# Four-layer graph network on one core: both edge counts inside the first sort, layer 0's gathers in three parts, its softmax by chunks

## The reference

```python
h = x @ W_lin + b_lin                         # 6250 x 128, 4 heads of 32
alpha = leaky_relu(h[src]·att_i + h[dst]·att_j + b_att, 0.2)   # 100000 x 4
amax = segment_max(alpha, src)
ex = exp(alpha - amax[src])
attn = ex / (segment_sum(ex, src) + 1e-16)    # softmax over the edges of one source
out = segment_sum(h[src] * attn, dst)
```

## Time and profile before

| | us |
|---|---|
| median of 3 runs | 8602.71 (8601.63 to 8605.87) |
| the profiled execution | 8623.17 |
| its span, first to last instruction | 8621.3 |

### The profile page before, as it was taken

One profiled execution on the slowest core, in us unless ns is written; L12 is line 12 of the kernel. 1 busy time (PEld: TensorE's weight loads), 2 busy tenths in 40 slices (PEclk: granted clock), 3 DMA queues, 4 the chain that ended last, 5 costly groups with the idle time before them and its releaser, 6 DMA issues. The chain is left out here.

```text
span 8621.3 us, 28596 instructions
## 1 busy us (share of the span) xinstructions
PE 941.1 (11%) x3526; PEld 575.1 (7%) x3526; DVE 4022.7 (47%) x9756; ACT 694.6 (8%) x1670; POOL 5185.7 (60%) x5176
## 2 busy tenths in 40 slices
PE   5301001310000000000004555100000001000000
PEld 4300000210000000000002222000000001000000
DVE  6881111954253443333333666667433335435445
ACT  0020000210000001000002333000000003000002
POOL 0077776023677675767664666663667775767673
PEclk9999999655555555555556877555555555555555
DMA  1070000000233333323232676431223331333332
GB/s 44 35 279 2 2 2 1 0 17 23 82 105 96 100 101 94 98 86 100 86 95 83 239 245 243 146 102 50 87 86 94 92 97 60 88 85 102 88 95 58
DMA packets 283027, 772.97 MB, mean 90 GB/s; under 512 B 112213, under 2 KB 116235, under 8 KB 269395
## 3 DMA queue, kind: packets, MB, share of 16 engines
q0 software_dynamic: 166160, 284.56, 14.7%
q1 hardware_dynamic: 98632, 378.76, 11.5%
q10 hardware_dynamic: 18040, 107.82, 3.2%
HBM read 359.19 MB, written 411.57 MB: 89 GB/s over the span
## 5 line engine op out<-in xcount | busy, mean ns | idle before, releaser
L569 POOL DMA_INDIRECT first_sj<-scores,prep_atdst x784 | 816.4, 1041 | 657.0 <-POOLq L59 401.1
L947 POOL DMA_INDIRECT l2z_rows<-proj,l2z_idx x784 | 786.9, 1004 | 425.6 <-issue 240.3
L1978 POOL DMA_INDIRECT l2s_krow<-table_k,l2s_idx x784 | 774.5, 988 | 417.1 <-issue 257.1
L947 POOL DMA_INDIRECT l3z_rows<-table,l3z_idx x784 | 791.2, 1009 | 339.1 <-issue 236.8
L947 POOL DMA_INDIRECT l1z_rows<-table,l1z_idx x784 | 786.5, 1003 | 327.1 <-issue 238.7
L947 POOL DMA_INDIRECT l0z_rows<-table,l0z_idx x784 | 776.3, 990 | 337.7 <-issue 232.3
L923 DVE SCALAR_TENSOR_TENSOR l2z_acc<-l2z_acc,g_dokeep,l2z_msg 128x128 f32<-128x128 f32 x784 | 278.4, 355 | 657.5 <-DVE l2z_acc L923 303.9
L923 DVE SCALAR_TENSOR_TENSOR l1z_acc<-l1z_acc,g_dokeep,l1z_msg 128x128 f32<-128x128 f32 x784 | 277.8, 354 | 591.6 <-DVE l1z_acc L923 291.6
L1933 PE MATMUL l2s_bank<-l2o_wr,l2s_fed 128*128 128x512 f32 x800 | 423.3, 690 | 300.8 <-ACT l2s_fed L1957 217.3
L1915 DVE SCALAR_TENSOR_TENSOR l2s_qrow<-l2s_qrow,g_dokeep,l2s_zrow 128x82 f32<-128x82 f32 x1568 | 368.0, 301 | 185.7 <-DVE l2s_qrow L1915 118.8
L923 DVE SCALAR_TENSOR_TENSOR l0z_acc<-l0z_acc,g_dokeep,l0z_msg 128x128 f32<-128x128 f32 x784 | 277.3, 354 | 274.5 <-DVE l0z_acc L923 148.6
(11 more groups left out here) (595 smaller groups left out, 3748.6 us busy)
## 6 DMA issues: line engine op xcount, KB each, us to landing
proj<-l2s_proj ACTq DMA_DIRECT2D x100, 1024.0 KB
spread_q<-prep_zero SPq DMA_DIRECT2D x98, 656.0 KB
l2s_zrow<-spread_q SPq DMA_DIRECT2D x98, 656.0 KB
prefix<-l3z_acc SPq DMA_DIRECT2D x98, 520.0 KB
prefix<-l0z_acc SPq DMA_DIRECT2D x98, 512.0 KB
prefix<-l1z_acc SPq DMA_DIRECT2D x98, 512.0 KB
prefix<-l2z_acc SPq DMA_DIRECT2D x98, 512.0 KB
first_sj<-scores,prep_atdst POOLq DMA_INDIRECT x784
```

The costliest lines, as they stand in the source:

```text
L569: nc.gpsimd.indirect_dma_start(out=sj[:, j, :], out_offset=None, in_=g.scores0, in_offset=bass.IndirectOffsetOnAxis(ap=at_dst[:, j:j + 1], ...
L947: nc.gpsimd.indirect_dma_start(out=rows[:, r, u, :], out_offset=None, in_=table, in_offset=bass.IndirectOffsetOnAxis(ap=idx[:, k * U + u:k ...
L1978: nc.gpsimd.indirect_dma_start(out=krow[:, h, u, :], out_offset=None, in_=g.table_k, in_offset=bass.IndirectOffsetOnAxis(ap=idx[:, h, u:u ...
```

## The change

1. **Counts.** Both tallies (`src` and `dst`) run in the first sort's turns, with rings of 2 (`RING2`) in place of 4. The digits, the zero memsets and the step table move from ahead of the network into its first turn (`later(0)`). Both raw arrays are loaded there. The second sort has no tally, no raw load and no digits.
2. **Loads in parts.** The 97 or 127 row loads are cut into 96 + 1 or 112 + 15 rows. The 96-row parts of `src` and `dst` don't wait for a memset. x goes by ACT's queue in parts of 96, 16 and 13 rows, the last two behind a memset that is now POOL's.
3. **Gathers of sj in three parts.** 560 columns (`BESIDE`) beside the second sort, 124 more (up to `SPREAD` = 684) at the start of a new block, then both spreads (100 scatters and 2 gathers), then the last 100.
4. **One block `source_softmax`** replaces the ten or so blocks between the second sort and the sum: positions, marks (forwards only), node ends, spreads, and a softmax with a running maximum and total by five chunks of columns (`FETCHED`), each when its gathers have landed. A scan within each partition gives running maxima; exp of the differences rescales the running total. `CarryStats` joins the partitions at the end: one row per partition is gathered from `stats`, corrected and scattered back. Then 50 node gathers in groups of 4. `table0` goes out in two parts, the first (h and si) at the block's start.
5. `ROW0` is 140 instead of 144; the scores si are stored too (`scores_i`); `stats` has 129 rows more; SP fills two more small tables (`rowed`).

The diff, cut to its core:

```diff
-ROW0 = 144
+ROW0 = D + 3 * HEADS
...
+RING2 = 2
...
+    def digits(self, eng, chain, key, hi, lo):
+        v = self.nc.vector
+        eng.wait_ge(*self.loaded)
+        chain(v.tensor_copy(key, self.raw))
+        rounded(v, chain, hi, key, 1.0 / NB, -(NB - 1) / 2.0 / NB)
+        chain(v.scalar_tensor_tensor(lo, hi, -float(NB), key, ALU.mult, ALU.add))
+        v.tensor_copy(self.hi[:], hi)
+        chain(v.tensor_copy(self.lo[:], lo))
...
-            if c >= 4:
-                eng.wait_ge(self.tallied, c - 3)
+            if c >= RING2:
+                eng.wait_ge(self.tallied, c - RING2 + 1)
...
+                nc.gpsimd.memset(g.x[96:P], 0.0).then_inc(cleared, 1)
+                pool.wait_ge(cleared, 1)
...
-                v.memset(g.zero[:], 0.0)
-                v.memset(g.x[96:P], 0.0).then_inc(ready, 1)
...
+                def later(t):
+                    if t == 0:
+                        v.memset(g.zero[:], 0.0).then_inc(ready, 1)
+                        v.memset(g.zmat[:], 0.0).then_inc(zeroed, 1)
+                        v.memset(g.eps[:], 1e-5)
+                        eng.wait_ge(io, 3)
+                        chain(v.tensor_copy(g.steps[:], isteps[:]))
+                        for tally in tallies:
+                            tally.digits(eng, chain, fkey[:], hi[:], lo[:])
+                    for tally in tallies:
+                        tally.offer(eng, t)
+
+                net.on_vector(eng, later)
...
+                flat = a["x"].rearrange("(p b) f -> p b f", b=NB)
+                act.dma_start(g.x[0:96], flat[0:96]).then_inc(nodes, 16)
+                act.wait_ge(cleared, 1)
+                act.dma_start(g.x[96:112], flat[96:112]).then_inc(nodes, 16)
+                act.dma_start(g.x[112:NREAL], flat[112:NREAL]).then_inc(nodes, 16)
...
+                for k in range(2):
+                    sp.dma_start(wide[0:96, k, :], load[k][0:96]).then_inc(edges, 16)
...
+                for k in range(2):
+                    by_row = arrays[k][0:EFULL * NC].rearrange("(p j) -> p j", j=NC)
+                    for lo, hi in ((0, 112), (112, EFULL)):
+                        sp.dma_start(raw[lo:hi, k, :], by_row[lo:hi]).then_inc(plain, 16)
...
+                sp.dma_start(by_nodes(g.scores_i), rows[:, :, D:D + HEADS]).then_inc(sis, 16)
...
-                for j in range(NC):
-                    nc.gpsimd.indirect_dma_start(out=sj[:, j, :], out_offset=None, in_=g.scores0,
-                                                 in_offset=bass.IndirectOffsetOnAxis(ap=at_dst[:, j:j + 1], axis=0)).then_inc(got[j % 2], 16)
-                for h in range(2):
-                    pool.wait_ge(got[h], 16 * NC // 2)
+                fetch_columns(nc, g, at_dst, sj, got, 0, BESIDE)
...
-                net.on_vector(eng, lambda t: tally.offer(eng, t))
-                tally.take(eng, count)
+                net.on_vector(eng, lambda t: None)
...
+FETCHED = [0, 392, 560, 684, 756, NC]
+BESIDE, SPREAD = 560, 684
+
+
+def fetch_columns(nc, g, at_dst, sj, got, lo, hi):
+    for c, (a, b) in enumerate(zip(FETCHED, FETCHED[1:])):
+        for j in range(max(a, lo), min(b, hi)):
+            nc.gpsimd.indirect_dma_start(out=sj[:, j, :], out_offset=None, in_=g.scores0,
+                                         in_offset=bass.IndirectOffsetOnAxis(ap=at_dst[:, j:j + 1], axis=0)).then_inc(got[c], 16)
...
+    def on_pool(self, pool):
+        where = self.order.lead_i
+        self.nc.gpsimd.indirect_dma_start(out=self.row[:], out_offset=None, in_=self.g.stats,
+                                          in_offset=bass.IndirectOffsetOnAxis(ap=where[:, 0:1], axis=0)).then_inc(self.lead, 16)
+        pool.wait_ge(self.fixed, 1)
+        self.nc.gpsimd.indirect_dma_start(out=self.g.stats, out_offset=bass.IndirectOffsetOnAxis(ap=where[:, 0:1], axis=0),
+                                          in_=self.row[:], in_offset=None).then_inc(self.sent, 16)
+        pool.wait_ge(self.sent, 16)
...
+            @block.gpsimd
+            def _(pool):
+                nc.gpsimd.iota(nid_i[:], pattern=[[1, NB]], base=EP, channel_multiplier=NB).then_inc(io, 1)
+                fetch_columns(nc, g, at_dst, sj, got, BESIDE, SPREAD)
+                for k, (order, table, node) in enumerate(((so, g.spread_s, lambda b: rows[:, b, D:D + HEADS]),
+                                                          (O.dst, g.spread_0, lambda b: rows[:, b, D + HEADS:D + 2 * HEADS]))):
+                    pool.wait_ge(named, k + 1)
+                    for b in range(NB):
+                        nc.gpsimd.indirect_dma_start(out=table, out_offset=bass.IndirectOffsetOnAxis(ap=order.start_i[:, b:b + 1], axis=0),
+                                                     in_=node(b), in_offset=None).then_inc(sent[k], 16)
+                for k, table in enumerate((g.scores_i, g.scores0)):
+                    nc.gpsimd.indirect_dma_start(out=init[:, k], out_offset=None, in_=table,
+                                                 in_offset=bass.IndirectOffsetOnAxis(ap=firsts[:, k:k + 1], axis=0)).then_inc(started[k], 16)
+                fetch_columns(nc, g, at_dst, sj, got, SPREAD, NC)
+                pool.wait_ge(stored, 16 * len(chunks))
+                carry.on_pool(pool)
+                for k, group in enumerate(GROUPS):
+                    for b in group:
+                        nc.gpsimd.indirect_dma_start(out=nodes[:, b, :], out_offset=None, in_=g.stats,
+                                                     in_offset=bass.IndirectOffsetOnAxis(ap=so.end_i[:, b:b + 1], axis=0)).then_inc(taken[k], 16)
...
+                for c, (lo, hi) in enumerate(chunks):
+                    m = hi - lo
+                    e, x0, x1 = sj[:, lo:hi, :], x[:, 0, 0:m], x[:, 1, 0:m]
+                    most, total = both[:, 1 + lo:1 + hi, HEADS:8], both[:, 1 + lo:1 + hi, 0:HEADS]
+                    if c == 2:
+                        eng.wait_ge(loaded[1], 16)
+                        eng.wait_ge(started[1], 16)
+                        for w in range(HEADS):
+                            chain.add(v.tensor_tensor_scan(sj_d[:, w, :], O.dst.keep[:], wide0[:, :, w], init[:, 1, w:w + 1], ALU.mult, ALU.add))
+                    eng.wait_ge(got[c], 16 * m)
+                    chain(v.tensor_tensor(e, e, si[:, lo:hi], ALU.add))
+                    chain(v.scalar_tensor_tensor(e, e, 0.2, e, ALU.mult, ALU.max))
+                    for w in range(HEADS):
+                        chain.add(v.tensor_tensor_scan(most[:, :, w], gap[:, lo:hi], e[:, :, w], both[:, lo, HEADS + w:HEADS + w + 1], ALU.add, ALU.max))
+                    chain.until()
+                    chain.add(v.tensor_tensor(x1, e, most, ALU.subtract))
+                    chain(v.tensor_tensor(x0, both[:, lo:hi, HEADS:8], bc_last(gap[:, lo:hi], HEADS), ALU.add))
+                    v.tensor_tensor(x0, x0, most, ALU.subtract).then_inc(asked, 1)
+                    eng.wait_ge(made, c + 1)
+                    for w in range(HEADS):
+                        v.tensor_tensor_scan(total[:, :, w], x0[:, :, w], x1[:, :, w], both[:, lo, w:w + 1], ALU.mult, ALU.add).then_inc(scanned, 1)
+                    eng.wait_ge(scanned, HEADS * (c + 1))
+                v.tensor_copy(ends[:], both[:, NC]).then_inc(known, 1)
+                carry.on_vector(eng, chain)
...
+                sp.dma_start(by_nodes(g.table0)[:, :, 0:D + HEADS], rows[:, :, 0:D + HEADS]).then_inc(half, 16)
+                for k, (table, wide) in enumerate(((g.spread_s, si), (g.spread_0, wide0))):
+                    sp.wait_ge(sent[k], 16 * NB)
+                    sp.dma_start(wide[:], table[0:EP, :].rearrange("(p j) w -> p j w", j=NC)).then_inc(loaded[k], 16)
+                stats = g.stats[0:EP].rearrange("(p j) w -> p j w", j=NC)
+                for c, (lo, hi) in enumerate(chunks):
+                    sp.wait_ge(scanned, HEADS * (c + 1))
+                    sp.dma_start(stats[:, lo:hi], both[:, 1 + lo:1 + hi]).then_inc(stored, 16)
+                for k, group in enumerate(GROUPS):
+                    b = span(group)
+                    sp.wait_ge(ready, k + 1)
+                    sp.dma_start(by_nodes(g.table0)[:, b, D + HEADS:ROW0], rows[:, b, D + HEADS:ROW0]).then_inc(tabled, 16)
```

More of the change, by code:

```diff
@@ L376, in pack, with sort_by_source @@
     chain(v.tensor_scalar(key, key, sign, None, ALU.mult))
-def sort_by_source(nc, g, a, wide, keys, rows, sjn, count, src_s, at_dst):
+def sort_by_source(nc, g, a, wide, keys, rows, sjn, raw, counts, src_s, at_dst):
     W8 = D + 2 * HEADS
@@ L384, in sort_by_source @@
     with Space(nc, "sa") as s:
-        raw = s.sb("raw", [P, 2, NC], I32)
         rest = s.sb("rest", [1, WIDE], I32)
@@ L484, in _, with count @@
                     mm.then_inc(pmd, 1)
-                net.on_tensor(pe, lambda t_: tally.count(pe, t_))
+                def count(t_):
+                    if t_ == 0:
+                        pe.wait_ge(zeroed, 1)
+                    for tally in tallies:
```

(15 more changed lines are left out.)

454 lines of the change are left out of this document (226 added, 228 removed).

## The result

The changed kernel takes **8269.05 us** (median of 4 runs, 8250.15 to 8279.79) where the kernel before took 8602.17 (4 runs, 8590.94 to 8605.87): a ratio of 0.9612, 95% interval 0.9593 to 0.9632, 333 us less. The forecast was 8182 us, in a range of 8040 to 8350. The sign, the size and the places were right; 88 of the forecast 421 us weren't gained, and the time lies above the 8110 to 8250 that the prediction gave to its own sum.

What follows compares the result with a forecast made beforehand. The second sort, slowed beside POOL's gathers, was the largest item ahead of the message sum. Sort end 1292 plus block 502 put its first gather at 1794 instead of 2214.9 us, minus 421: 8182 us, range 8040 to 8350.

Steps and rivals of the forecast that it cites:

- its own sum: Whole kernel: the prediction's main case, 8182 us, over 8110 to 8250; chance 0.36.
- Start: Ahead of the first sort's first turn: earlier loads let DVE take it at about 122 us, not 175.81; minus 54.
- the rule on engines for a row count: Loads: a transfer uses the largest number up to 16 dividing its outer dimension; x's tail then takes 1 us, not 13.
- Second count in the first sort: First sort: 43 more batches, 70 us, plus 8 us for rings of two; the sort ends at S = 428 us.
- Second sort: From S, the first sort's end, to the second sort's end: 864 us, ending at 1292 instead of 1822.6.
- I take PE's turns as covered: Second sort's slow stretch: PE seems to hold a store of some 80 instructions, so only DVE's copies are charged.
- the slow pace: Beside POOL's unbroken gathers: DVE starts one instruction per 1.40 us, stages 7.00 us apart; PE likewise.
- rival 1: Second sort: the slow pace doesn't come back, POOL's 560 gathers set the end, 135 us earlier; 8050 us; chance 0.2.
- rival 2: Second sort: turns not covered, some ten at 45 us each; plus 150, 8330 us; chance 0.24.
- New block: From the second sort's end to layer 0's first message-sum gather: POOL is the spine, 502 us.
- rival 3: New block: every gather beside DVE goes at 1.40 us, 49 us more; 8231 us; chance 0.12.
- Message sums, no change: Layer 0's message sum, 1114 us: POOL's issue bounds it, so nothing gained; a shift may move it 30 either way.

Runs made afterwards that it cites:

- the run with 672 beside: Changed kernel with 672 instead of 560 gathers beside the second sort: 7432.66 us, 0.9781 of before, on chip 2; 8186.94 us, 0.9542, on chip 1.
- the softmax run: Changed kernel with DVE waiting for all gathers of sj ahead of the first softmax chunk: 8334.89 us, 0.9639 of before, on chip 0.

## Why the prediction was right, step by step

It forecast minus 421 us at the first gather of the message sum and minus 333.2 was measured. The first sort, the second and the new block all came out longer than forecast, so no large errors cancelled. By its own steps:

- **Start: right, 3 us late.** First turn at 125.12 us for 122. The cover was as forecast: the network's 55 stages were done at 102.6, PE's loop over x at 114, and 12 us of memsets and digits lay between. The edges came later than forecast (packing at 26.09, not 13, behind the landing of `sa_rest`), and it didn't matter, since PE's loop ended last. What ended PE's first wait was the last of the weights, at 27.35 us, and x was there when PE came to it at 29.3. So the loads of x in parts didn't bind, and the rule on engines for a row count, which would have had x earlier by 12 us, was neither confirmed nor refuted.
- **Second count in the first sort: 8 us undersized.** 305 us from the first turn to the copies of the counts, 297 forecast (219 before plus 78). That is 16.6 us beyond the 70 us of batches, 1.3 us a turn, not 0.6. The idle times of DVE that the trace puts down to the two rings add up to 8.5 us (26 waits); where the rest of it lies isn't shown. With the 3 us above, the second sort begins 12 us later than S = 428, at 439.9.
- **Second sort: 52 us undersized**, 916 for 864. This is the step that failed: "I take PE's turns as covered". (A reading ahead of it was wrong too: the slow pace doesn't begin 209 us after the first gather but after some 90 to 110, and the normal stretch behind it is a pause's doing. The number came out because both kernels have nearly the same mixture there, 245 and 246 instructions; that was luck. It takes away what rival 1 had for it, "preceded by 209 normal us", and the bound of a network "as fast as in 404 to 613" is no clean network.) The slow stretch itself was as forecast (it ended at S+786, forecast S+775; 26 us behind the last gather). But PE had no store left in a turn. One turn, by PE's record and by the engines that take its results:

```profile
821.13 1.97 PE L267 MATMUL sd_turn<-g_ident,prep_key 128*128 128x128 f32 x8 [20.19 <-issue]
...
826.32 0.75 DVE L222 TENSOR_SCALAR prep_key<-sd_turn,g_signs 128x512 f32<-128x512 f32 x1 [2.87 <-remote]
837.45 0.75 DVE L222 TENSOR_SCALAR prep_key<-sd_turn,g_signs 128x512 f32<-128x512 f32 x1 [10.38 <-remote]
...
847.95 0.59 ACT L292 COPY prep_wide<-sd_pturn 128x512 f32<-128x512 f32 x1 [27.57 <-remote]
859.15 0.59 ACT L292 COPY prep_wide<-sd_pturn 128x512 f32<-128x512 f32 x1 [10.61 <-issue]
...
860.97 0.73 DVE L252 COPY_PREDICATED prep_pay<-sd_mask,prep_wide 128x512 f32<-128x512 int32 x1 [20.75 <-issue]
862.20 0.68 DVE L238 TENSOR_TENSOR sd_mask<-prep_key 128x512 f32<-128x512 f32 x1
...
877.79 0.68 DVE L238 TENSOR_TENSOR sd_mask<-prep_key 128x512 f32<-128x512 f32 x1
882.95 0.69 DVE L238 TENSOR_TENSOR sd_mask<-prep_key 128x512 f32<-128x512 f32 x1 [1.50 <-remote]
889.95 0.69 DVE L238 TENSOR_TENSOR sd_mask<-prep_key 128x512 f32<-128x512 f32 x1 [1.50 <-remote]
```

  The four halves of the turn reach their takers at 826.32, 837.45, 847.95 and 859.15: 11.1, 10.5 and 11.2 us apart, and a half is four transposes and four weight loads, 8 x 1.40 = 11.2 us. PE's own record shows its first eight in 1.97 us and hides this: the takers' starts show when a result is there. So rival 2's price (45 us for a turn's 32 instructions) holds for the turn back. Its sum of plus 150 doesn't, because a wait isn't all lost: behind it DVE starts six stages at full pace (862.20 to 877.79, 3.1 us apart) before it falls to 7.00 again (882.95, 889.95), as if the instructions it didn't get had been laid up. In the slow stretch five pairs of turns, with the stages between them, took 73 us each; the same five took 15 to 29 us on chip 2, where nothing slows (the run with 672 beside). The truth lay between the sum and rival 2.
- **New block: 24 us undersized**, 526 for 502. The last 100 gathers took 137 us and not 125, and the carry 19.8 us and not 9, at the upper of its two bounds. The 12 us lie in the first 40 or so of the gathers, beside the dense chunks of the softmax (the contention of rival 3: 12 of its 49 us). Taking the chunks away didn't win them back, though, since the gathers then went at the slow pace. Chunk, store and the tail came out within 6 us. The 145 instructions of DVE lay beside POOL as forecast; the wait for `named` never bound.
- **Message sums, no change**: right for layer 0's, 1114 us in both. The part behind the first gather is 6406 us before and 6367 after in the profiled executions, 40 us less where 30 were allowed; but before's was 20 us above its median and after's 19 below, so the medians leave nothing of it.

12 + 52 + 24 = 88 us, the whole difference. Rival 1 (no slow pace) didn't happen on the chip of the result. On chips 2 and 6 there is no slow pace at all and the kernel before is 1000 us faster; the forecast's range holds for one kind of chip only, the kind that the profile of before came from.

## What to carry to other kernels

When one queue issues small DMAs without a pause for hundreds of microseconds, look in the other engines' timelines for starts at a constant pitch: there an instruction costs the same whatever its size, so move away the work that has many small ones (a count of 64 matmuls) and leave what has few large ones. A stage with such a stretch should be compared by where its milestones lie, since its length wanders by 15 us and more from run to run, as much as a real edit is worth. And measure a reorder on a second chip before it is kept: undoing the counts' move costs 120 us on chip 0, and the move by itself costs 72 us on chip 2. A mean pace over a window can hide two paces: look at the starts one by one before a rule is read from it.

## What the runs showed of the hardware

- **Chips differ in this.** On chips 2 and 6 the kernel before takes 7605 and 7603 us and on the others 8587 to 8646. The rows of layer 1's message sum, which the change doesn't touch, on chip 2 (first, the run with 672 beside) and on chip 0 (the kernel before):

```profile
L846 POOL DMA_INDIRECT l1z_rows<-table,l1z_idx x784 | 751.1, 958 | 247.7 <-issue 238.6
```

```profile
L947 POOL DMA_INDIRECT l1z_rows<-table,l1z_idx x784 | 790.1, 1008 | 325.1 <-issue 234.3
```

  784 gathers take 999 us (751.1 + 247.7) there and 1115 us here. Why two of the chips don't show it, what it is that fills up, and whether the recording of an execution has a part in it were not tried.
- **The pace comes from the gathers, heals in a pause, and is shared.** Without gathers none (540 us for 786 instructions); with a pause of 6 to 7 us it is gone for about 50 us (594 to 650 in the changed kernel, 564 to 614 in the one before); and with nothing else running POOL itself falls to 1.39 us a gather.
- **A gather beside a dense DVE can be held up for 92.56 us.** Every hold of over 5 us in these traces lies within four gathers of a stop of POOL: behind a rest that was put in (chip 1, and 88.51 us on chip 2) or behind POOL's own pause of 6 to 7 us (24.87 and 27.88 us on chip 0, the softmax run; one of 27.9 us in each of three runs on chips 2 and 6). The stop isn't enough: in the changed kernel and the one before, POOL makes the same pause, and no gather beside the sort took over 2 us. What else it takes isn't shown. On chip 2, 672 beside, 5 us behind a pause of 7.13 us:

```profile
601.53 27.90 POOL L1797 DMA_INDIRECT first_sj<-scores,first_atdst  x1 [0.30 <-issue]
```
